# An int8 cross attention on one core: exponentials without biases, and the clamp moved from VectorE to ScalarE

## The reference, cut to what matters

```python
def _fq(x, delta, zp, n_bits):
    xi = _round_ste(x / delta) + zp
    xq = jnp.clip(xi, 0.0, 2.0 ** n_bits - 1.0)
    return (xq - zp) * delta

sim = jnp.einsum('bhid,bhjd->bhij', _fq(q, dq, 128.0, 8), _fq(k, dk, 128.0, 8)) * SCALE
attn = jax.nn.softmax(sim, axis=-1)
out = jnp.einsum('bhij,bhjd->bhid', _fq(attn, dw, 0.0, 8), _fq(v, dv, 128.0, 8))
out = out.transpose(0, 2, 1, 3).reshape(b, n, D)
return out @ wo + bo
```

## Time and profile before

| | us |
|---|---|
| median of 3 runs | 985.18 (985.14 to 994.31) |
| the profiled execution | 987.16 |
| its span, first to last instruction | 985.3 |
| a2 alone, first maximum to first product of f0 | 208.0 to 313.5 |

### The profile page before, as it was taken

The page is one execution under the profiler, slowest core; times in us unless marked ns, Lnnn a source line. Parts: engine busy times, 40 slices in busy tenths (PEclk is TensorE's granted clock), DMA queues, the critical chain, the costliest instruction groups (busy, mean ns, idle before and its releaser), DMA issues.

```text
span 985.3 us, 23673 instructions
## 1 busy us (share of the span) xinstructions
PE 858.5 (87%) x8603; PEld 522.0 (53%) x8603; DVE 737.6 (75%) x1592; ACT 627.1 (64%) x1551; POOL 552.0 (56%) x1069
## 2 busy tenths in 40 slices
PE   4988888865666878999999899999889989999996
PEld 1444444433334545555766456555556557676765
DVE  5788888768894755566657667767647887999987
ACT  1899999968885213554355455655546577786874
POOL 2788888856652423764445565656435363646533
PEclk9999999777785989999999899999999999999999
DMA  9500000000000000000000001000000000000000
GB/s 267 175 1 2 0 0 2 1 1 1 1 2 1 1 0 1 2 2 2 1 1 3 18 25 26 22 24 24 2 1 3 1 2 2 2 7 7 7 7 22
DMA packets 23579, 16.48 MB, mean 17 GB/s; under 512 B 8744, under 2 KB 20400, under 8 KB 23344
## 3 DMA queue, kind: packets, MB, share of 16 engines
q1 hardware_dynamic: 23472, 15.06, 5.3%
HBM read 10.85 MB, written 1.05 MB: 12 GB/s over the span
## 4 chain that ended last, share of the span: by engine, by line
PE 55%; DVE 21%; ACT 13%; issue 6%; POOL 3%; SPq 1%; DMA 1%; DVEq 0%; ACTq 0%; POOLq 0%
ACT sb_E L1276 10%; PE ps_context L799 5%; PE ps_context L802 4%; PE ps_scores L899 3%; PE ps_scores L875 3%; PE ps_turned L713 2%; PE ps_scores L752 2%; PE ps_scores L792 2%; PE ps_turned L1176 2%; PE ps_turned L1114 2%; PE ps_turned L1177 2%; PE ps_turned L1178 2%; PE ps_scores L1155 2%; PE ps_scores L1153 2%; PE ps_scores L1154 2%
## 5 line engine op out<-in xcount | busy, mean ns | idle before, releaser
L1276 ACT ACTIVATE sb_E<-ps_scores,sb_neg_max,sb_score_scale 128x256 f32<-128x256 f32 (+1 forms) x384 | 191.0, 514 | 21.7 <-DVE sb_neg_max L1577 15.9
L2337 POOL TENSOR_SCALAR sb_E<-sb_E,sb_inv_sum 128x256 f16<-128x256 f32 x256 | 123.8, 483 | 27.5 <-DVE sb_inv_sum L1613 7.8
L1529 ACT ACTIVATE sb_E<-ps_scores,sb_ff_bias 128x512 f32<-128x512 f32 x128 | 88.1, 691 | 45.0 <-PE ps_scores L1155 41.5
L1784 DVE TENSOR_REDUCE sb_neg_half<-ps_scores 128x16 f32<-128x1024 f32 x48 | 58.7, 1222 | 63.9 <-PE ps_scores L875 63.9
L1596 DVE TENSOR_REDUCE sb_neg_quad<-ps_scores 128x2 f32<-128x512 f32 (+1 forms) x96 | 64.3, 684 | 42.0 <-PE ps_scores L754 30.0
L713 PE MATMUL ps_turned<-sb_ident 128*128 128x512 f16 x289 | 86.5, 419 | 9.4 <-DVE sb_ident_b L2202 9.4
L1304 ACT ACTIVATE sb_E<-ps_scores 128x512 f32<-128x512 f32 x96 | 57.2, 598 | 47.8 <-PE ps_scores L794 46.6
L1401 ACT ACTIVATE sb_E<-ps_scores 128x1024 f32<-128x1024 f32 x48 | 49.2, 1024 | 54.1 <-PE ps_scores L907 54.1
L1572 DVE TENSOR_REDUCE sb_neg_raw<-ps_scores 128x4 f32<-128x1024 f32 x64 | 77.8, 1216 | 7.4 <-PE ps_scores L685 7.2
L2270 POOL TENSOR_SCALAR sb_veps<-sb_mv 128x2 f32<-128x2 f32 x72 | 19.8, 275 | 112.6 <-DVE sb_mv L1554 111.8
L1276 ACT ACTIVATION_READ_ACCUMULATOR sb_E<-ps_scores,sb_neg_max,sb_score_scale 128x1 f32 x384 | 79.1, 206 | 0.0
(11 more groups left out here) (302 smaller groups left out, 2589.8 us busy)
## 6 DMA issues: line engine op xcount, KB each, us to landing
sb_moe_up<-in_moe_up SPq DMA_DIRECT2D x1, 2048.0 KB
sb_KS<-sb_qk_parts SPq DMA_DIRECT2D x96, 16.0 KB, 1.8
sb_QS<-sb_qk_parts SPq DMA_DIRECT2D x96, 16.0 KB, 1.8
sb_rows<-in_rows SPq DMA_DIRECT2D x1, 1216.0 KB, 7.2
out_x<-sb_raw_context SPq DMA_DIRECT2D x8, 128.0 KB, 1.8
sb_X<-in_x SPq DMA_DIRECT2D x1, 768.0 KB, 9.3
sb_square<-in_square SPq DMA_DIRECT2D x1, 768.0 KB, 10.7
sb_ctxT<-in_ctxT SPq DMA_DIRECT2D x1, 512.0 KB, 11.1
```

Source lines behind the costliest of these rows:

```text
L1276: last = act.activation(E[:, ring, head], SC[t % 2][:, head], ACT.Exp, bias=neg_max[:, ring, h:h + 1], scale=scale, accum_out=row_sum[:, r ...
L1529: last = act.activation(U_full[:, n % RING, :], banks[n % 4], ACT.Gelu, bias=bias, scale=1 / WEIGHT_SCALE)
L1784: dve.tensor_reduce(neg_half[:, n % 2, :, :, :].rearrange("p x i g -> p (x i g)"), SC[0][:, :].rearrange("p (h k) -> p h k", k=CTX), AX.X, ...
L2337: last = pool.tensor_scalar(E16[:, ring, SEQ * h:SEQ * h + SEQ], E[:, ring, SEQ * h:SEQ * h + SEQ], inv_sum[:, ring, h:h + 1], HALF, ALU.m ...
```

## The change

In a2, VectorE now subtracts the maxima of all sixteen heads from the whole score tile (1024 columns instead of 512), ScalarE takes one exponential over 1024 elements, and VectorE sums all of them (2048 elements for a pair of units instead of 1024). The eight exponentials with a bias and the scaled maxima go.

The clamp moves to ScalarE, as a rectifier. The rounding writes 1280 - p instead of 1024 + p. After the transpose a rectifier with bias 255 - 1280 gives max(255 - p, 0). PE multiplies that with the values and adds, with the same weights, the product with a constant tile of -255, so that the result is minus the clamped product; the output scale is negated. So each of the eight value products of a unit is followed by a second one.

The reading of round T (the transposed input, into `hT`) moves to ScalarE as well. The rounding is moved from unit t-2 to unit t-3 in ScalarE's step t, and the order of its step is: context, exponential, casts, `hT`, clamp, rounding. The wait of the subtraction for the rounding of unit n-4 stays as it was. The score tile is free for PE when the subtraction has read it. Three more small setup instructions fill the constants.

```diff
@@ quant_scores (PE)
-                wait(pe, S["exped_half"], B["exped_half"] + n - 1)
+                if L.over_self:
+                    wait(pe, S["exped_half"], B["exped_half"] + n - 1)
+                elif n < 2:
+                    pe.wait_ge(S["exped"], B["exped"] + n - 1)
+                else:
+                    pe.wait_ge(S["subbed"], B["subbed"] + n - 1)
...
-                        if g:
-                            wait(pe, S["subbed"], B["subbed"] + n - 1)
@@ quant_values (PE)
-                                         stop=(j == 1 and (u % 4 == 3 or not L.over_self)), skip_group_check=True)
+                                         stop=(j == 1 and u % 4 == 3 and L.over_self), skip_group_check=True)
+                        if not L.over_self:
+                            last = pe.matmul(CO[32 * g:32 * g + 32, at:at + P], value, neg_qmax[:, :], start=False,
+                                             stop=(j == 1), skip_group_check=True)
@@ quant_exps (ACT)
-                scale = score_scale[:, 0:1] if L.name == "a1" else score_scale[:, 1:2]
+                if not L.over_self:
+                    act.wait_ge(S["subbed"], B["subbed"] + n + 1)
+                    act.activation(E[:, ring, :], E[:, ring, :], ACT.Exp, scale=score_scale[:, 1:2])\
+                       .then_inc(S["exped"], 1)
+                    return
...
-                for h in range(L.heads if L.over_self else BIASED):
...
-                if not L.over_self:
-                    act.wait_ge(S["subbed"], B["subbed"] + n + 1)
-                    rest = E[:, ring, CTX * BIASED:]
-                    last = act.activation(rest, rest, ACT.Exp, scale=scale)
@@ ACT
+            def land(L, B, p, t):
+
+                t -= L.lag
+                n, ring = L.steps * p + t, t % 2
+                if not live(n, L.units):
+                    return
+                wait(act, S["valued"], B["valued"] + n - 1)
+                act.wait_ge(S["turned"], B["turned"] + n + 1)
+                act.activation(PT16[:, ring, :], TP[t % 2][:, :].bitcast(F16), ACT.Relu, bias=clamp[:, 0:1]).then_inc(S["landed"], 1)
+
             def round_off(L, B, p, t):
 
-                n, ring = L.steps * p + t - 2, (t - 2) % 4
-                if not live(n, L.units) or L.over_self:
+                n, ring = L.steps * p + t - 3, (t - 3) % 4
+                if not live(n, L.units):
                     return
                 act.wait_ge(S["normed"], B["normed"] + n + 1)
                 wait(act, S["turned"], B["turned"] + n - 3)
-                act.activation(E16[:, ring, :], E[:, ring, :], ACT.Copy, bias=HALF).then_inc(S["rounded"], 1)
+                act.activation(E16[:, ring, :], E[:, ring, :], ACT.Copy, bias=HALF + 256.0, scale=-1.0)\
+                   .then_inc(S["rounded"], 1)
+
+            def quant_hT(L, B, p, t):
+
+                for j, items in enumerate(L.rounds[t % L.per_batch]):
+                    batch, b, at = L.batch(p, t, "T"), L.batch(0, t, "T") % 2, L.round(p, t, j)
+                    if [kind for kind, _ in items] == ["T"] and live(batch) and at is not None:
+                        act.wait_ge(S["round_done"], B["round_done"] + at[0] + 1)
+                        act.activation(hT[:, b, :], RD[:, 0:SEQ], ACT.Identity, bias=col(L.name + "_b"),
+                                       scale=col(L.name + "_g")).then_inc(S["round_free"], 1)
@@ quant_step (ACT)
                 quant_take_context(L, B, p, t)
                 quant_exps(L, B, p, t)
+                if L.over_self:
+                    return
+                if t % L.per_batch == 0:
+                    cross_casts(L, B, p, t)
+                quant_hT(L, B, p, t)
+                land(L, B, p, t)
                 round_off(L, B, p, t)
-                if not L.over_self and t % L.per_batch == 0:
-                    cross_casts(L, B, p, t)
@@ quant_maxima (DVE)
-                    dve.tensor_reduce(neg_raw[:, ring, 0:L.heads], src, AX.X, ALU.max).then_inc(S["raw_max"], 1)
-                    dve.wait_ge(S["raw_max"], B["raw_max"] + n + 1)
-                    dve.tensor_scalar(neg_max[:, ring, 0:BIASED], neg_raw[:, ring, 0:BIASED], neg_scale[:, 1:2], None,
-                                      ALU.mult).then_inc(S["maxed"], 1)
+                    dve.tensor_reduce(neg_raw[:, ring, 0:L.heads], src, AX.X, ALU.max).then_inc(S["maxed"], 1)
+                    dve.wait_ge(S["maxed"], B["maxed"] + n + 1)
                     wait(dve, S["rounded"], B["rounded"] + n - 3)
-                    dve.tensor_tensor(E[:, ring, CTX * BIASED:].rearrange("p (h k) -> p h k", k=CTX), src[:, BIASED:, :],
-                                      neg_raw[:, ring, BIASED:, None].to_broadcast([P, H - BIASED, CTX]),
-                                      ALU.subtract).then_inc(S["subbed"], 1)
+                    dve.tensor_tensor(E[:, ring, :].rearrange("p (h k) -> p h k", k=CTX), src,
+                                      neg_raw[:, ring, :, None].to_broadcast([P, H, CTX]), ALU.subtract)\
+                       .then_inc(S["subbed"], 1)
@@ invert_sums (DVE)
-                    dve.tensor_reduce(row_sum[:, ring, BIASED:], E[:, ring, CTX * BIASED:].rearrange(
-                        "p r (h k) -> p r h k", k=CTX), AX.X, ALU.add).then_inc(S["row_summed"], 1)
+                    dve.tensor_reduce(row_sum[:, ring, :], E[:, ring, :].rearrange("p r (h k) -> p r h k", k=CTX), AX.X,
+                                      ALU.add).then_inc(S["row_summed"], 1)
@@ quant_land and round_of (DVE)
-                if not live(n, L.units):
+                if not live(n, L.units) or not L.over_self:
                     return
...
+                if items[0][0] == "T" and not L.over_self:
+                    return
@@ setup (DVE)
+                link(dve.memset(clamp[:, :], QMAX - HALF - 256.0))
+                link(dve.memset(neg_qmax[:, :], -QMAX))
...
+                link(dve.tensor_scalar(out_scale[:, 1:2], out_scale[:, 1:2], -1.0, None, ALU.mult))
```

More of the change, by code:

```diff
@@ L259 @@
 EXP1, EXP2 = 3, 18
-BIASED = 8
 HI_BY_VECTOR = 1
@@ L312, in counts @@
     c.update(scored=n, maxed=n, exped=n, raw_sum=n // 2, summed=n // 2, normed=n, turned=n, landed=n, valued=n,
-             keyed=NBATCH, exped_half=n)
-    c["scaled_max" if layer.over_self else "raw_max"] = n
-    if not layer.over_self:
+             keyed=NBATCH)
+    if layer.over_self:
+        c.update(scaled_max=n, exped_half=n)
+    else:
         c.update(subbed=n, row_summed=n // 2, rounded=n, q_cast=NBATCH, v_cast=NBATCH)
@@ L457, in build @@
         minus_half = sb("minus_half", [P, 4])
+        clamp = sb("clamp", [P, 1])
+        neg_qmax = sb("neg_qmax", [P, P], F16)
         ctxT = sb("ctxT", [P, NBATCH, 2, CTX])
@@ L625, in build @@
         N_LOADS = {k: 16 * len(v) for k, v in LOADS.items()}
-        V_SETUP = 20
+        V_SETUP = 23
         block = ctx.enter_context(nc.Block())
@@ L1264, in quant_exps @@
                     return
-                scale = score_scale[:, 0:1] if L.name == "a1" else score_scale[:, 1:2]
-                act.wait_ge(S["maxed"], B["maxed"] + n + 1)
-                if L.over_self:
-                    act.activation(neg_max[:, ring, 0:L.heads], neg_raw[:, ring, 0:L.heads], ACT.Copy, scale=score_scale[:, 0:1])\
-                       .then_inc(S["scaled_max"], 1)
-                used = "normed" if L.over_self else "rounded"
-                wait(act, S[used], B[used] + n - 3)
-                if L.over_self:
-                    act.wait_ge(S["scaled_max"], B["scaled_max"] + n + 1)
-                for h in range(L.heads if L.over_self else BIASED):
+                if not L.over_self:
[3 more added lines that the diff above has]
+                    return
+                act.wait_ge(S["maxed"], B["maxed"] + n + 1)
+                act.activation(neg_max[:, ring, 0:L.heads], neg_raw[:, ring, 0:L.heads], ACT.Copy, scale=score_scale[:, 0:1])\
+                   .then_inc(S["scaled_max"], 1)
+                wait(act, S["normed"], B["normed"] + n - 3)
+                act.wait_ge(S["scaled_max"], B["scaled_max"] + n + 1)
+                for h in range(L.heads):
                     head = slice(L.keys * h, L.keys * h + L.keys)
                     last = act.activation(E[:, ring, head], SC[t % 2][:, head], ACT.Exp,
-                                          bias=neg_max[:, ring, h:h + 1], scale=scale,
+                                          bias=neg_max[:, ring, h:h + 1], scale=score_scale[:, 0:1],
                                           accum_out=row_sum[:, ring, h:h + 1])
-                    if h == (1 if L.over_self else BIASED - 1):
+                    if h == 1:
                         last.then_inc(S["exped_half"], 1)
-                if not L.over_self:
-                    act.wait_ge(S["subbed"], B["subbed"] + n + 1)
-                    rest = E[:, ring, CTX * BIASED:]
-                    last = act.activation(rest, rest, ACT.Exp, scale=scale)
```

## The result

The kernel with the change took 1003.88 us (median of five, 1002.57 to 1006.75) against 985.18 for the one before. The medians differ by 18.7 us, a ratio of 1.0190. The prediction was 1004.2. The profiled execution took 1003.24 us with a span of 1001.3.

A forecast was written before the change was run, and what follows sets the result against it. VectorE was taken to set a2's pace before, the wait for ScalarE's rounding after. Terms 0.2 + 13.6 + 5.0 + 0.2 = +19.0 us on the 985.2 median give 1004.2, with an 8-in-10 range of 994 to 1013.

The forecast's parts named there:

- The deciding wait: In a2, subtraction n waits for the rounding of n-4, now behind exponential n-1; batch 15.45 us for 12.93; forecast 71%.
- The waits of VectorE: In a2, VectorE idles ahead of each subtraction for ScalarE's rounding: about 2.2 us in even units, 1.2 in odd.
- From unit 4 to 14: Five batches of a2, put at 13.7, 14.3 and three times 15.45: 74.4 us for 60.8, so +13.6.
- From unit 14 to f0: End of a2 to f0's first product: 11.0 us to the last subtraction, 30.1 in all for 25.1, so +5.0.
- The first four units: Units 0 to 3 of a2 have no such wait; wider subtractions and sums against work removed: +0.2 us.
- The prices: ScalarE's costs start to start in a2: exponential 1.04 us, read of T 0.46, clamp 1.04 (ends 0.63 and 1.2).
- Sixteen value products: PE's doubled products in a2: 0.3 us more at full clock, 0.7 at half, hidden by waits except at the end.
- VectorE's list decides: Rival in a2: the wait is no limit; a batch takes 11.8 us, 978 in all; 9%.
- The wide subtraction is blocked by GpSimd: Rival in a2: GpSimd's multiplication holds the subtraction up to 1.4 us in each odd unit; +8, 1012 us; 7%.
- PE keeps its full clock through round 1: Rival in a2: V and G at twice the clock give back 0.85 us a batch; -6, 998 us; 8%.
- Another table: Rival in a2: the rectifier needs another table, two 1.28 us loads in each of 16 units; +41, 1045 us; 3%.
- everything behind a2 as merely shifted: Work behind a2 is untouched by the change, so it moves by the same time as a2's end.

The follow-up runs named there:

- e1: The kernel after with ScalarE's rounding of unit t-3 moved ahead of the exponential in its step; 986.50 us, ratio 0.9965 to the kernel before.
- e8: The kernel before with only the rounding of unit t-3 in place of t-2 in ScalarE's step t; 1001.23 us, ratio 1.0124 to before.
- e4: The kernel after with the clamp back on VectorE, constant products kept; 995.07 us, ratio 1.0066 to the kernel before.
- e7: The kernel before with only the wide exponential, its subtraction and sums; 996.35 us, ratio 1.0077 to the kernel before.
- e11: The kernel after without the constant products on PE, so outputs lack that term; 1009.20 us, ratio 1.0216 to the kernel before.
- e9: The kernel before plus 12 filling multiplications on PE ahead of round 1 in five even steps; 982.62 us, ratio 0.9939 to before.
- e12: The kernel after, unchanged, run once more; 1008.49 us, ratio 1.0191 to the kernel before.
- e6: e5 plus 12 filling multiplications on PE ahead of round 1 in five even steps; 982.18 us, ratio 0.9929 to the kernel before.
- e5: The kernel after with the rounding ahead of the exponential and the casts at the step's end; 984.87 us, ratio 0.9970 to before.

## Why the prediction was right

**The deciding wait.** It was named with its place, and e1 and e8 show it to be the cause. The prediction's terms for one batch, beside the same intervals of the profile after, from the subtraction at 273.94 to the one at 289.24:

| interval | predicted | measured |
|---|---|---|
| even subtraction to the sums | 1.80 | 1.82 |
| sums, scaling, inverse | 2.84 | 2.83 |
| quantised queries and keys, to V | 0.72 | 0.63 |
| V and G, until VectorE reads | 1.69 | 1.69 |
| to the casts | 0.71 | 0.71 |
| casts; clamp; rounding and signal | 0.54; 1.04; 1.15 | 0.55; 1.01; 1.15 |
| odd subtraction and signal | 1.27 | 1.26 |
| exponential; read of T | 1.04; 0.46 | 1.05; 0.45 |
| clamp; rounding and signal | 1.04; 1.15 | 2.15 together |
| sum | 15.45 | 15.30 |

The waits of VectorE, put at 2.2 and 1.2, were 2.40 and 1.03. What remained of GpSimd's blocking was put right too: the subtraction and the next maximum read PSUM and are not held up (beside GpSimd's multiplication from 226.53 to 228.43 the maximum at 227.63 took its usual 1.22 us).

**The stage.** From unit 4 to 14 it was 74.1 us for 74.4. Of its five batches (even maxima at 227.63, 241.63, 255.57, 270.31, 285.62, 301.76) the first two took 14.0 and 13.9 for the predicted 13.7 and 14.3, and the others 14.7, 15.3 and 16.1 for three times 15.45: their mean was hit, not each one. The last of them ends with 0.91 us in which the next maximum waited for its scores, which the prediction doesn't have:

```profile
301.76 1.23 DVE L1604 TENSOR_REDUCE sb_neg_raw<-ps_scores 128x16 f32<-128x1024 f32 x1 [0.91 <-PE ps_scores L697]
```

Counted from even subtraction to even subtraction, which is the circle itself, the five are 14.1, 14.1, 15.3, 15.3 and 14.9 us.

From unit 14 to f0 it was 30.5 us for 30.1: 10.6 for 11.0 to the last subtraction, and 20.0 for 19.1 behind it. The first four units, put at 0.2 longer, took 19.57 us as before. In all a2 grew by 18.7 for 18.8 predicted of it. That it came out to 0.1 is luck in part, for the parts miss by 0.2, 0.3 and 0.4 us in both directions. The 0.2 us for the setup can't be seen: a2 starts at 208.06 in place of 208.01.

**The prices.** The clamp was put at 1.04 from start to start and took 1.01 (1.10 for itself): of the ends 0.63 and 1.2 the nearer rows of ScalarE itself were the right guide. The Trainium skill (ScalarE: Activation LUTs, Rules for kernel authors) wants rectifiers on VectorE; in this kernel's own order e4 agrees with it by 10.9 us of a2. But e7 and e1 show that it can't be read by the instruction's duration alone: with the clamp on VectorE and no wait for the rounding, a2 is 110.5; with the clamp (and T) on ScalarE and the rounding first, it is 104.1.

**One term was too large.** Sixteen value products were put at 0.3 us more than eight at full clock. In pairs they took 0.42 us (274.44 to 274.86) against 0.29 for eight, so 0.13 more; the transposes just ahead took 0.62 and 0.61 us, so the clock was alike. e11, without them, gains 0.7 us in all of a2.

**The rivals.** *VectorE's list decides* (978 us): false of this kernel, as the 2.40 and 1.03 us show, but it describes e1's batch of 11.84 us, for which it gave 11.8. Yet its a2 was to be 7.4 us shorter than before, and e1's is 1.4 shorter. The rival took 1.1 us off in each of five batches. Before the change the scaled maximum was blocked only in the last three of them (for 1.63, 1.62 and 1.62 us; 0.23 in the first two), so in the first two the list grows, and e1's take 12.0 and 11.3 us for 11.6 and 10.9; of the last three (12.8, 11.8, 12.2 for 12.95, 12.93, 12.48) only one gained the 1.1. *The wide subtraction is blocked by GpSimd*: false. In the timeline of both engines the subtraction at 284.33 ran its usual 1.23 us beside GpSimd's 1.90 from 283.60; at the end of a2 the operation from SBUF to SBUF was blocked, as in the earlier trace rows: 1.90 us for two that take 0.67 at 281.51:

```profile
283.60 1.90 POOL L2373 TENSOR_TENSOR sb_E<-sb_E,sb_inv_sum 128x1024 f32<-128x1024 f32 x1
...
308.90 1.90 POOL L2373 TENSOR_TENSOR sb_E<-sb_E,sb_inv_sum 128x1024 f32<-128x1024 f32 x1 [1.80 <-DVE sb_inv_sum L1640]
308.90 0.42 DVE L1683 TENSOR_TENSOR sb_X<-ps_rounds,sb_X 128x256 f32<-128x256 f32 x1
309.24 1.90 DVE L1589 TENSOR_SCALAR sb_z<-sb_X,sb_mv,sb_rstd 128x128 f32<-128x128 f32 x2
```

*PE keeps its full clock through round 1*: false (0.80 and 1.06); e9 shows its mechanism: 0.71 us a batch at VectorE's wait, where 0.85 was put. *Another table*: false. Between the exponentials and clamps of a2 there is no load; ScalarE's timeline shows the next one behind the last clamp, for f0:

```profile
331.88 1.11 ACT L1452 ACTIVATE sb_VCTX<-ps_turned,sb_clamp 128x1024 f16<-128x1024 f16 x1 [1.78 <-PE ps_turned L712]
333.01 1.28 ACT L1527 ACT_TABLE_LOAD   x1
```

**What was right by luck in part.** The prediction took everything behind a2 as merely shifted. By profile the rest was 2.8 us shorter after than before, so the profiled executions differ by 16.1 us and not by the 19.0 forecast of them; over the experiments the rest moved by up to 7.6 us. The medians differ by 18.7 us here, the means of the same runs by 16.2, and the medians of e12's series by 20.9. That 1003.88 lies 0.3 us from 1004.2 is luck; what the mechanism gives is a2, 18.7 us for 18.8.

## What to carry to other kernels

Where a buffer of a ring is freed by the last item of an engine's step, and that step begins by waiting for the engine which needs the buffer, the two engines take turns: look for such a circle before counting work, and move the freeing item ahead of the waiting one (20 us of a2 here, with no instruction changed). Work taken off the fullest engine paid here only once no circle of waits was longer than its list. And where PE stands idle for microseconds ahead of multiplications on the path, look at what filling that idle time does before rebuilding anything: here two added lines gave more than the rebuilt stage in its best order (a2 at 99.1 against 103.8 us, 0.6 against 0.3% under the kernel before).

## What was not expected of the hardware

**The filled idle time.** In e6 and e9 the granted clock over a batch was 1.00, and in the kernel before it was 0.74; the stretch of e9's batch, in the order of the columns above:

```profile
263.79:274.87 11.08, 8.93 (x68) 4.73 (x68) 9.87 (x23) 10.55 (x42) 7.70 (x14) 1.00 0.00 1
```

PE's round 1 gives back some 0.7 us a batch by VectorE's wait (1.74 to 1.03). The larger part came through the scaled maximum, as the expectation of e9 had it: it starts at 272.97, 0.27 us ahead of GpSimd's multiplication (273.24), where before it started 0.31 us behind it, and takes 0.34 in place of 1.62. The two together are 2.0 us, and the batch gained 1.85. In e6, which has no scaled maximum, the gain over e5 comes in part from elsewhere: VectorE's maxima wait less for their scores. The views of waits of e5 and of e6:

```profile
DVE sb_neg_raw L1605 <- PE ps_scores L697: 5.4, 6, 1.6
DVE sb_neg_raw L1607 <- PE ps_scores L697: 2.1, 4, 0.9
```

**The rest changes between executions.** The work behind a2 is the same instructions in all of these kernels but took 669.0 to 676.6 us of the span. The time ahead of a2 moved as well, from 207.2 to 211.5. The two profiles of the kernel after show where. From f0's first product to a table load on ScalarE 184 us later they differ by 0.4 us (183.98 and 184.37), and to the next one by 3.4 (470.00 and 473.42). The granted clock differs in between. This is the stretch from 240 to 350 us behind f0's first product, in the profile after:

```profile
572.30:682.30 110.00, 105.91 (x1181) 62.57 (x1182) 76.37 (x161) 62.16 (x123) 66.23 (x181) 0.98 0.10 24
```

The same stretch of e12, the same kernel:

```profile
575.17:685.17 110.00, 107.38 (x1168) 63.01 (x1164) 74.82 (x159) 60.87 (x122) 63.86 (x175) 0.95 0.10 24
```

0.98 became 0.95. In the first 50 us behind f0's first product it was 0.92 in both. What makes the clock come out one way or the other stays open; no run here was made for it, and the series ran on different chips (e1 to e4, e5 to e11, and e12). The medians of one kernel moved between series by 0.35% for the one before (985.2 to 988.7) and 0.46% for the one after (1003.9 to 1008.5). The reading here went by a2, which agreed to 0.2 us in the one kernel that was profiled twice.
